# One fused attention and mixture-of-experts kernel: gate scores a slot later, shared tiles two pairs later, three row scatters a slot, and expert rows weighted before they are scattered

## The reference

```python
# attention: 8 heads, each with two score maps over 8 features
scores = einsum('bqhif,bkhif->ibhqk', q, k) * 8 ** -0.5
att = softmax(scores)[0] - diff_weight * softmax(scores)[1]
o = einsum('bhqk,bkhe->bqhe', att, v)
attn = (rmsnorm(o) * norm_w) @ Wo.T + bo                  # times 1 - diff_weight
# experts: one shared, 8 routed, the two best by sigmoid gate
gates = sigmoid(xn @ Wg);  vals, idx = top_k(gates, 2);  vals /= vals.sum()
shared = silu(xn @ Ws1) * (xn @ Ws3) @ Ws2
routed = sum over the two experts of vals * (silu(xn @ We1) * (xn @ We3) @ We2)
out = x + attn + (shared + routed) / 3
```

## Time and profile before

| what | value |
|---|---|
| three timed runs | median 591.58 us (591.34 to 592.21) |
| the profiled execution | 593.5 us, span from first to last instruction 591.4 us |
| busy | PE 563.0, DVE 469.2, ACT 401.8, POOL 218.2 us |
| granted TensorE clock, mean | 0.983 of full speed |
| DMA queues | 74.07 MB, mean 125 GB/s; HBM read 40.08 MB, written 15.80 MB |
| scatters to xs and to yt | 64 and 72, each about 1 us of POOL |

### The profile page before, as it was taken

The page is one execution under the profiler, slowest core; times in us unless marked ns, Lnnn a source line. Parts: engine busy times, 40 slices in busy tenths (PEclk is TensorE's granted clock), DMA queues, the critical chain, the costliest instruction groups (busy, mean ns, idle before and its releaser), DMA issues.

```text
span 591.4 us, 13553 instructions
## 1 busy us (share of the span) xinstructions
PE 563.0 (95%) x4688; PEld 335.1 (57%) x4688; DVE 469.2 (79%) x1012; ACT 401.8 (68%) x808; POOL 218.2 (37%) x296
## 2 busy tenths in 40 slices
PE   7797999999999999999999999999999999999993
PEld 6565545555555554555665665566556655665442
DVE  5989778888888896778878787887878788878195
ACT  4463575767667666777777777777677777777781
POOL 5630063555655554123323233332333233332310
PEclk9898898999999999999999999999999999999998
DMA  6997400260116222485435834476344844420292
GB/s 181 206 154 151 110 6 15 55 150 29 37 37 151 59 84 58 133 215 179 130 109 150 264 111 122 130 203 196 116 144 128 231 140 150 130 83 14 66 298 81
DMA packets 62531, 74.07 MB, mean 125 GB/s; under 512 B 7296, under 2 KB 42496, under 8 KB 62464
## 3 DMA queue, kind: packets, MB, share of 16 engines
q1 hardware_dynamic: 57952, 64.00, 42.1%
q0 software_dynamic: 4352, 8.95, 4.7%
q10 hardware_dynamic: 160, 0.26, 0.2%
HBM read 40.08 MB, written 15.80 MB: 94 GB/s over the span
## 4 chain that ended last, share of the span: by engine, by line
PE 67%; DVE 14%; issue 7%; DMA 3%; ACT 3%; POOL 3%; SPq 2%; POOLq 0%; DVEq 0%; ACTq 0%
PE O L1167 15%; PE T L1138 10%; PE F L1207 9%; DVE rowmax L846 7%; PE F L1221 6%; PE F L1204 5%; PE T L1143 4%; PE F L1101 2%; PE O L1128 2%; PE F L1186 2%; DMA yt<-ysb,xst 2%; SPq L264 1%; DVE base L938 1%; PE O L1033 1%; DVE base L924 1%
## 5 line engine op out<-in xcount | busy, mean ns | idle before, releaser
L652 ACT ACTIVATE probs<-T 128x512 f32<-128x512 f32 x372 | 202.7, 597 | 94.9 <-PE T L1143 61.7
L846 DVE TENSOR_REDUCE rowmax<-S 128x1 f32<-128x512 f32 x370 | 237.9, 682 | 27.9 <-PE S L1128 25.9
L1128 PE MATMUL S<-kop,qop 32*128 32x512 f32 x370 | 140.5, 454 | 3.4 <-DVE rowmax L846 2.1
L1167 PE MATMUL O<-probs,vop 128*32 128x512 f32 x1024 | 124.1, 601 | 0.2
L486 POOL DMA_INDIRECT yt<-ysb,xst x72 | 72.1, 1001 | 136.6 <-DMA yt<-ysb,xst 119.7
L1138 PE MATMUL T<-qop,kop 32*128 32x512 f32 x372 | 99.4, 498 | 1.4 <-ACT probs L652 1.0
L1143 PE MATMUL T<-mop,ones_r 2*128 2x512 f32 x372 | 78.3, 399 | 0.0
L475 POOL DMA_INDIRECT xs<-xn,slot_i x64 | 62.5, 977 | 42.1 <-DVE rowmax L846 26.1
L652 ACT ACTIVATE probs<-V 128x512 f32<-128x512 f32 x126 | 76.5, 607 | 1.9 <-PE S L1143 1.9
L1207 PEld LDWEIGHTS F<-xsT,wrt_all 128*128 128x128 f32 x576 | 67.0, 191 | 13.3 <-issue 8.8
L1207 PE MATMUL F<-xsT,wrt_all 128*128 128x128 f32 x576 | 73.9, 281 | 0.5
(11 more groups left out here) (168 smaller groups left out, 879.1 us busy)
## 6 DMA issues: line engine op xcount, KB each, us to landing
wrt_all<-in_wexp SPq DMA_DIRECT2D x72, 384.0 KB, 3.9
qop<-qparts SPq DMA_DIRECT2D x64, 128.0 KB
kop<-kparts SPq DMA_DIRECT2D x62, 128.0 KB
xs<-xst SPq DMA_DIRECT2D x12, 387.0 KB, 7.9
xst<-xs SPq DMA_DIRECT2D x36, 129.0 KB, 3.9
base<-in_x SPq DMA_DIRECT2D x8, 256.0 KB, 4.8
xn<-yt SPq DMA_DIRECT2D x8, 256.0 KB, 4.8
out_x<-base SPq DMA_DIRECT2D x7, 256.0 KB, 3.8
```

The source lines that it names most:

```text
L652: A(probs[:, n % NP, :], banks[e_bank[n]][:, :], ACT.Exp, scale=SCALE).then_inc(s_p, 1)
L846: V.reduce_max(rowmax[hf][:, x_map[n], c, x_row[n]:x_row[n] + 1], banks[x_bank[n]][:, :], AX).then_inc(s_mx, 1)
L1128: mm(banks[x_bank[n]][:, :], qop[b % 2][at:at + BAND, c, t * P:(t + 1) * P], kop[b % 2][at:at + BAND, c, :], start=True, stop=True, tile_p ...
L1167: last = mm(O[VW * j:VW * (j + 1), :], vop[b % 2][:, t, (4 * g + j) // MAPS, :], probs[:, n % NP, :], start=(t == 0), stop=(t == QT - 1), ...
```

## The change

1. `Z_AT` from (-7, -3) to (-6, -2); the filler of slot -8 uses bank F1 in place of V.
2. VectorE's first routing steps stand behind every second row maximum in place of every one; `do_prefix` moves from pair 2 to 3, and GpSimd's steps from slots 4 and 6 to 7 and 9. The five steps that compute the weights move from the end of the chain into its middle.
3. Shared tiles take pairs 6 to 21. Pairs 4 and 5 are bare with 24 fillers each, pairs 20 and 21 are not bare any more; pairs 59 to 63 have no filler.
4. Row scatters begin in slot 12 and come three in a slot.
5. Each row of `xs` carries the token's weight beside its number (`W` from 129 to 130). `copy_y` becomes two ScalarE instructions of 128x128 that multiply by it, and each scatter to `yt` waits for its own half. `combine` becomes two plain VectorE additions of 128x512 for each sequence, in place of eight of 128x128 with weights.
6. Partition p holds the four consecutive tokens 4p to 4p+3 of a sequence, in place of tokens p, p+128 and so on. A partition's part of x, of the output and of one choice in `yt` is then one run of 2 KB, in place of four of 512 bytes, and `load_y` is one DMA per sequence.

```diff
-    SH_AT = [8 + 2 * i for i in range(SH_TILES)]
+    SH_AT = [12 + 2 * i for i in range(SH_TILES)]
-    Z_AT = [-7, -3]
-    PREFIX_AT = 2
-    SCAT0 = 10
+    Z_AT = [-6, -2]
+    PREFIX_AT = 3
+    SCAT0, SCATS = 12, 3
+    FILL_TO, HEAVY = 59, 6
-    W = D + 1
+    W = D + 2
...
-        R_HOT, R_IDX, R_LOAD, R_STEPS = 14, 33, 36, 41
-        R_DVE = {n: n for n in range(14)} | {19: 28, 20: 29} | {n: n + 5 for n in range(29, 41)}
-        R_POOL = {n: 4 if n < 19 else 6 for n in (14, 15, 16, 17, 18, 21, 22, 23, 24, 25, 26, 27, 28)}
+        R_HOT, R_IDX, R_LOAD, R_STEPS = 14, 38, 41, 41
+        R_DVE = {n: 2 * n if n < 14 else n + 13 for n in range(19)} | {24: 36, 25: 37} | {n: 46 + (n - 34) // 2 for n in range(34, 41)}
+        R_POOL = {n: 7 if n < 24 else 9 for n in (19, 20, 21, 22, 23, 26, 27, 28, 29, 30, 31, 32, 33)}
...
-                sp.dma_start(base[:, QT * b:QT * b + QT, :], x_in[b].rearrange("(t p) d -> p t d", p=P)).then_inc(s_x[b], 16)
+                sp.dma_start(base[:, QT * b:QT * b + QT, :], x_in[b].rearrange("(p t) d -> p t d", p=P)).then_inc(s_x[b], 16)
...
-                for k in range(TOPK):
-                    at = TOKENS * k + SEQ * b
-                    sp.dma_start(gbuf[b][:, k, :, :], yt[at:at + SEQ, :].rearrange("(t p) d -> p t d", p=P)).then_inc(s_g[b], 16)
+                rows = yt[0:TOPK * TOKENS, :].rearrange("(k b p t) d -> b p k (t d)", k=TOPK, b=BATCH, p=P)
+                sp.dma_start(gbuf[b].rearrange("p k t d -> p k (t d)"), rows[b]).then_inc(s_g[b], 16)
...
-                G.iota(xn[:, :, D:W].bitcast(i32), pattern=[[P, NT], [0, 1]], base=TOKENS * k, channel_multiplier=1).then_inc(s_ids, 1)
+                ids = xn[:, :, D:D + 1].bitcast(i32).rearrange("p (b t) o -> p b (t o)", t=QT)
+                G.iota(ids, pattern=[[SEQ, BATCH], [1, QT]], base=TOKENS * k, channel_multiplier=QT).then_inc(s_ids, 1)
+                G.tensor_scalar(xn[:, :, D + 1], wts[:, k, :], 1.0, None, ALU.mult).then_inc(s_ids, 1)
...
             def scatter_y(r, i):
+                gp.wait_ge(s_yc, 2 * r + i + 1)
                 if i == 0:
-                    gp.wait_ge(s_yc, r + 1)
                     gp.wait_ge(s_xl[r % NX], 16 * (r // NX + 1))
...
-                    for i in range(2):
+                    for i in range(SCATS):
                         if scat < TOPK * NT:
-                            gp.wait_ge(s_mx, 4 * (slot + LEAD) + 3 + 2 * i)
+                            gp.wait_ge(s_mx, 4 * (slot + LEAD) + 3 + i)
                             scatter(scat)
                             scat += 1
...
-                A(ysb[r % 2][:, :, :].rearrange("p s d -> p (s d)"), F[1][:, 0:TOK], ACT.Copy).then_inc(s_yc, 1)
+                for i in range(2):
+                    A(ysb[r % 2][:, i, :], F[1][:, i * P:(i + 1) * P], ACT.Copy, scale=xst[r % NX][:, i, D + 1:W]).then_inc(s_yc, 1)
...
-                dve.wait_ge(s_g[b], 16 * TOPK)
-                dve.wait_ge(s_rt, R_STEPS)
+                dve.wait_ge(s_g[b], 16)
...
+                rows = base[:, QT * b:QT * b + QT, :]
                 for k in range(TOPK):
-                    for t in range(QT):
-                        if k:
-                            dve.wait_ge(s_cmb, 8 * b + t + 1)
-                        row = base[:, QT * b + t, :]
-                        V.scalar_tensor_tensor(out=row, in0=gbuf[b][:, k, t, :], scalar=wts[:, k, QT * b + t:QT * b + t + 1],
-                                               in1=row, op0=ALU.mult, op1=ALU.add).then_inc(s_cmb, 1)
+                    if k:
+                        dve.wait_ge(s_cmb, TOPK * b + k)
+                    V.tensor_tensor(rows, rows, gbuf[b][:, k, :, :], ALU.add).then_inc(s_cmb, 1)
...
-                    keep_busy(LEAD_FILL, ["F0"] if slot < -9 else ["V"])
+                    keep_busy(LEAD_FILL, ["F0"] if slot < -9 else ["F1"] if slot == -8 else ["V"])
...
-                if bare(p):
-                    keep_busy(8 if p < 4 else 4, ["F1"])
+                if bare(p) and p < FILL_TO:
+                    keep_busy(8 if p < HEAVY else 4, ["F1"])
...
-                if bare(p):
-                    keep_busy(16 if p < 4 else 8, ["F1"])
+                if bare(p) and p < FILL_TO:
+                    keep_busy(16 if p < HEAVY else 8, ["F1"])
```

More of the change, by code:

```diff
@@ L325, in load_y @@
                     sp.wait_ge(s_st, 4 * QUADS * (BATCH - 1))
-                for k in range(TOPK):
-                    at = TOKENS * k + SEQ * b
-                    sp.dma_start(gbuf[b][:, k, :, :], yt[at:at + SEQ, :].rearrange("(t p) d -> p t d", p=P)).then_inc(s_g[b], 16)
+                rows = yt[0:TOPK * TOKENS, :].rearrange("(k b p t) d -> b p k (t d)", k=TOPK, b=BATCH, p=P)
+                sp.dma_start(gbuf[b].rearrange("p k t d -> p k (t d)"), rows[b]).then_inc(s_g[b], 16)
             def store_out(n):
-                sp.wait_ge(s_cmb, 8 * (n + 1))
-                sp.dma_start(out[n].rearrange("(t p) d -> p t d", p=P), base[:, QT * n:QT * n + QT, :]).then_inc(s_out, 16)
+                sp.wait_ge(s_cmb, TOPK * (n + 1))
+                sp.dma_start(out[n].rearrange("(p t) d -> p t d", p=P), base[:, QT * n:QT * n + QT, :]).then_inc(s_out, 16)
             def store_last(h):
@@ L336, in store_last @@
                 sp.wait_ge(s_pd, QT * n + t0 + 2)
-                sp.dma_start(out[n, P * t0:P * t0 + 2 * P].rearrange("(t p) d -> p t d", p=P),
+                sp.dma_start(out[n].rearrange("(p t) d -> p t d", p=P)[:, t0:t0 + 2, :],
                              base[:, QT * n + t0:QT * n + t0 + 2, :]).then_inc(s_out, 16)
@@ L360, in _ @@
             sp.dma_start(wsh[:, :], wexp[E]).then_inc(s_wsh, 16)
-            sp.wait_ge(s_pz, 1)
+            sp.wait_ge(s_pz, 2)
             sp.wait_ge(s_ids, 1)
@@ L471, in scatter @@
                     row_ids(k)
-                    gp.wait_ge(s_ids, k + 2)
+                    gp.wait_ge(s_ids, 2 * k + 3)
                 if n >= 2:
@@ L809, in route @@
                     V.reduce_max(rank2, cand[:, :, :], AX).then_inc(s_rt, 1)
-                if n == 36:
+                if n == 14:
                     V.tensor_tensor(total, max1, max2, ALU.add).then_inc(s_rt, 1)
-                if n == 37:
+                if n == 15:
                     V.tensor_scalar(total, total, 2.0 * (SHARED + TOPK), None, ALU.mult).then_inc(s_rt, 1)
-                if n == 38:
+                if n == 16:
                     V.reciprocal(inv, total).then_inc(s_rt, 1)
-                if n == 39:
+                if n == 17:
                     V.tensor_tensor(wts[:, 0, :], max1, inv, ALU.mult).then_inc(s_rt, 1)
-                if n == 40:
+                if n == 18:
                     V.tensor_tensor(wts[:, 1, :], max2, inv, ALU.mult).then_inc(s_rt, 1)
-                if n == 19:
+                if n == 24:
                     V.tensor_tensor(cnt[:, :, :], over(scan[1][:, 2 * NT - 1, :], CMAX),
                                     step128[:, :].unsqueeze(1).to_broadcast([P, E, CMAX]), ALU.is_gt).then_inc(s_rt, 1)
-                if n == 33:
+                if n == 38:
                     V.tensor_tensor(jge[:, :, :], over(jrow[:, :], E),
                                     ecnt[1][0:1, E:2 * E].unsqueeze(1).to_broadcast([1, PIECES, E]), ALU.is_ge).then_inc(s_rt, 1)
-                if n == 20:
+                if n == 25:
                     V.reduce_sum(ecnt[0][:, E:2 * E], cnt[:, :, :], AX).then_inc(s_rt, 1)
-                if n == 29:
+                if n == 34:
                     V.reduce_sum(pos1, hot1[:, :, :], AX).then_inc(s_rt, 1)
-                if n == 30:
+                if n == 35:
                     V.reduce_sum(pos2, hot2[:, :, :], AX).then_inc(s_rt, 1)
-                if n == 31:
+                if n == 36:
                     V.tensor_copy(slot_i[:, 0, :], pos1).then_inc(s_rt, 1)
-                if n == 32:
+                if n == 37:
                     V.tensor_copy(slot_i[:, 1, :], pos2).then_inc(s_rt, 1)
-                if n == 34:
+                if n == 39:
                     V.reduce_sum(jexp[:, :], jge[:, :, 0:E - 1], AX).then_inc(s_rt, 1)
-                if n == 35:
+                if n == 40:
                     V.tensor_copy(jidx[:, :], jexp[:, :]).then_inc(s_rt, 1)
@@ L1216, in down @@
                 else:
-                    claim(["F1"], s_yc, r + 1)
+                    claim(["F1"], s_yc, 2 * (r + 1))
                 pe.wait_ge(s_hid, j + 1)
@@ L1249, in _ @@
                 if -9 < slot < -2:
-                    keep_busy(LEAD_FILL, ["V"])
+                    keep_busy(LEAD_FILL, ["F1"] if slot == -8 else ["V"])
                 if slot == -1:
```

27 lines of the change are left out of this document (14 added, 13 removed).

## The result

The changed kernel took 615.64 us (median of 4 runs, 610.86 to 617.21). The kernel before took 591.89 us in the same comparison (591.34 to 602.16). The ratio on record is 1.0375, 95% interval 1.033 to 1.042 (the two medians alone give 1.040): slower, as forecast, but by 24 us in place of 6.7, and outside the range of 586 to 604. The profiled execution took 617.21 us with a span of 615.4, against 593.5 and 591.4 before.

A forecast was written before the change was run, and what follows sets the result against it. TensorE, busy for 95% of the span, was taken as the bound. Terms +17.8 (wait at pair 17) - 1.3 - 0.4 - 2.0 - 3.2 + 0.4 - 5.0 + 0.4 = +6.7 on 591.58, about 598.0 us; range 586 to 604.

The forecast's parts named there:

- the quick pace: Row scatters on GpSimd, three a slot: 1.56 us each when no other DMAs are in flight.
- Rival 1: GpSimd's scatters come 1.34 us apart, wait at pair 17 about 2 us, time 582.5 us; chance 0.10.
- the 105.4 of the sum: GpSimd's first row scatter, slot 12, starts at 105.4 us; sum to the end of `unpack` gives 218.6.
- the tail term: Pairs 59 to 63 without filler -3.2 us, reciprocal no longer behind `combine` -1.8; sum -5.0, bounds -2 and -7.
- TensorE's filler was free: Tail: the bound of -2 us on the -5.0 term, if removing filler gains nothing.
- rival 4: Without filler the tail falls to 1.2 GHz: +10 us, 608 us; chance 0.04.
- the 7.5, 8.3 and 8.1 us: Forecast lengths of pairs 4, 5 and 6: 23.9 us in place of 27.07, so -3.2 us.
- `combine` and the reciprocal: Tail: `combine` falls from 17 to 9.6 us, so the last reciprocal stops waiting, 1.8 us gained.
- the lead and the x rows: Before pair 0: moved `do_z` and filler -1.3 us; first x load in 2 KB rows -0.4 us.
- the routing gain: Pairs 0 to 3: VectorE's routing steps spread out, sum -2.0 us, bounds 0 and -4.
- pair 0 perhaps keeping its clock: Within the routing term: -0.8 us for a chance that pair 0 stays at 2.4 GHz, worth -2.
- 11.1 us of gains: Whole kernel: the forecast's gains alone, without the wait at the end of pair 17 and its low clock.

The follow-up runs named there:

- the run with four in flight: Changed kernel with four semaphores for the row scatters in place of two, so each waits for the last but three; still three a slot: 596.03 us, ratio 1.0077.
- the best version: Changed kernel, two scatters a slot, filler back in pairs 59-63, 24 fillers in pair 58, three last routing steps later, eight fillers in pair 6: 587.03 us, ratio 0.9858.

## Why the prediction was right and wrong

**Right: the direction and its main cause.** TensorE waits at the end of pair 17 for `unpack`, behind scatters that land too slowly. I gave 1.56 us as the quick pace; ten undisturbed ones made 1.51. The wait was 17.2 in place of 15.8, and the low clock behind it cost 2.6, not 2. Rival 1 ("GpSimd keeps up") needed a pace below 1.45; the run with four in flight shows that it would have come with 1.26, and with no wait at all where I had left 2.

**Luck in that term.** The end of `unpack` was forecast for 218.6 in the clock of the kernel before, in which TensorE ends pair 17 at 203.30; the changed kernel ends it 2.66 earlier. In that clock the measured end, 217.75, is 220.4, so 1.8 later than forecast, and TensorE was ready 0.5 later. GpSimd's first scatter:

```profile
100.96 1.25 POOL L477 DMA_INDIRECT xs<-xn,slot_i  x1 [0.30 <-POOL xn L464]
```

That is 103.6 in the old clock, 1.8 before the 105.4 of the sum. From it to the end of `unpack` it took 116.8 us, where 113.2 were counted. The two errors half cancel. Some of the 3.6 lies in stretches where the scatters came slower than 1.56 (119.28, 121.22, 123.16, 125.34 are 1.9 to 2.2 apart); how it divides was not worked out.

The Trainium skill's rule (DMA: Bandwidth & Descriptors, "Anatomy of one DMA — SWDGE (gpsimd) path"), 2.15 us for such a DMA by the estimate in the prediction, is not borne out: two in flight at 1.51 apart make a round trip of 3.0 us, and the profiles with four in flight and with two a slot give 3.0 and 3.1 us as the median from issue to landing of the scatters to `yt`. Only the shortest of them, 2.2 us, come near it.

**Failed: the tail term.** The step reads "fillers of pairs 59 to 63: eight take 0.55 net, four 0.33 ... so -3.2". The trace shows +8.5 over pairs 58 to 63 in its place. The step has two faults. First, it priced the filler as work on TensorE's path. Where the clock holds, the filler costs almost nothing: four pairs without it are 0.2 us shorter together. The forecast had named this as a bound ("TensorE's filler was free"). Second, it gave the filler no effect on the clock. That mechanism stood in the list as rival 4, with a chance of 0.04, turned down because "TensorE has no long gap there". The clock does not need a long gap here: the earlier trace rows already had 89 to 92 with TensorE 2.83 of 3.00 busy and the clock at 0.60, and the `up` of 3.67 us in the earlier trace rows was a fall without one.

How much of the +8.5 is the filler's depends on what the clock does before it. Pair 58, which keeps its 12 fillers, loses 2.4 us in each profile of a changed kernel that falls there. Over pairs 58 to 63 taking the filler out costs 4.7 us in the kernel before, 2.7 with two a slot (41.4 against 38.7), 1.2 with 24 fillers in pair 58 (37.3 against 36.1), and 0.6 in the changed kernel itself (44.1 against 43.5). In none of the four is it a gain.

**Failed: pairs 4 to 6.** Of the 7.5, 8.3 and 8.1 us the first two held (7.4 and 8.0) and pair 6 did not (11.4). I took the fall in pair 4 for the price of the first shared tile and let the move remove it. The kernel before with its tiles moved shows the fall at the same place without a tile. The change also spread the routing steps up to pair 6, and the fall went with them; with two edits there pair 6 takes 8.1 us and the term comes out at -3.6.

**Small terms.** The ScalarE copies cost 0.15 (forecast 0.4), `combine` and the reciprocal gave 2.0 (1.8), pairs 19 to 22 cost 0.2 (0.4, for 20 to 22). The start as a whole gave 2.6 of 3.7, by luck: the lead and the x rows gave 3.1 (1.7), and from the first exp to pair 3 it took 0.5 more in place of 2.0 less. No execution shows the routing gain: that stretch is 34.8 to 35.3 us long in the nine profiles with the new start and 34.5 to 35.2 in the five with the old one. The forecast had counted 0.8 for pair 0 perhaps keeping its clock, and in the changed kernel the clock was down there for longer than before. How much of the rest the clock took was not worked out.

So the forecast counted 11.1 us of gains, and 3.2 of them, the filler's, are not there at any clock. The clock took back 3.4 in pair 6. The profile of the best version is 5.3 us shorter than that of the kernel before: 1.7 by pair 3, 3.6 in pairs 4 to 6 and 2.0 behind the last product, less 2.0 that it loses between pair 6 and pair 63.
